# A gated cross-attention stack on one core: scaled scores, the order of the 4-bit minima, a weight split in a tail, and an earlier first query

## The reference, cut to what matters

```
x = x + tanh(g_xattn[i]) * xattn_i(layernorm(x), ctx)
x = x + tanh(g_ffn[i])   * ffn_i(layernorm(x))
```

## Time and profile before

| | |
|---|---|
| median of 3 runs | 2156.29 us (2155.64 to 2157.31) |
| the profiled execution | 2155.29 us; span 2153.5 us from first to last instruction |
| mean granted clock of PE | 0.968 |
| busy, share of the span | PE 92%, DVE 69%, ACT 48%, POOL 44% |
| chain that ended last | PE 64%, DVE 18%, ACT 9%, issue 7%, POOL 1% |
| first layer's attention, loop | about 46 to 588 us |
| third layer's attention | about 1119 to 1490 us |
| third feed-forward | about 1490 to 1524 us |

### The profile page before, as it was taken

The page is one execution under the profiler, slowest core; times in us unless marked ns, Lnnn a source line. Parts: engine busy times, 40 slices in busy tenths (PEclk is TensorE's granted clock), DMA queues, the critical chain, the costliest instruction groups (busy, mean ns, idle before and its releaser), DMA issues.

```text
span 2153.5 us, 33307 instructions
## 1 busy us (share of the span) xinstructions
PE 1971.2 (92%) x10874; PEld 1651.7 (77%) x10874; DVE 1475.5 (69%) x2725; ACT 1029.6 (48%) x2264; POOL 938.5 (44%) x971
## 2 busy tenths in 40 slices
PE   5999999999748999998988999997799999999997
PEld 4788888888636888887666888886678888888886
DVE  5777787777777887887334555656467766677676
ACT  3666666666514544553123544542155555545552
POOL 2555554554445665664321323322144444444432
PEclk9999999999978999999988999999899999999999
DMA  3222221122211111111210101001101110111001
GB/s 140 57 64 75 77 85 57 61 74 67 92 34 40 63 65 54 52 45 64 67 54 4 34 8 34 23 1 55 54 11 47 47 46 11 50 45 45 14 23 45
DMA packets 47070, 106.77 MB, mean 50 GB/s; under 512 B 6065, under 2 KB 21937, under 8 KB 43105
## 3 DMA queue, kind: packets, MB, share of 16 engines
q1 hardware_dynamic: 46944, 105.14, 15.3%
HBM read 98.37 MB, written 6.75 MB: 49 GB/s over the span
## 4 chain that ended last, share of the span: by engine, by line
PE 64%; DVE 18%; ACT 9%; issue 7%; POOL 1%; DVEq 0%; ACTq 0%; POOLq 0%
PE psX L369 23%; PE psQ L369 11%; PE psS L369 11%; PE psO L369 10%; PE psT L752 5%; DVE pT_lo L909 2%; ACT pT_hi L1092 1%; DVE dq_space L461 1%; DVE nmax L897 1%; ACT dq_space L448 1%; DVE p_sb L891 1%; DVE nbias L895 1%; PE psT L369 1%; ACT p_sb L1085 1%; DVE qscr L470 1%
## 5 line engine op out<-in xcount | busy, mean ns | idle before, releaser
L1202 POOL TENSOR_SCALAR p_sb<-p_sb,rrec 128x512 f32<-128x512 f32 (+1 forms) x320 | 266.0, 831 | 704.1 <-DVE rrec L905 704.0
L1092 ACT ACTIVATE pT_hi<-psT 128x512 fp32r<-128x512 f32 (+2 forms) x384 | 235.0, 612 | 336.9 <-PE psT L752 336.0
L909 DVE TENSOR_TENSOR pT_lo<-psT,pT_hi 128x512 fp32r<-128x512 f32 (+2 forms) x384 | 271.4, 707 | 81.9 <-ACT pT_hi L1092 81.9
L369 PE MATMUL psO<-pT_hi,v_hi 128*128 128x256 f32 (+1 forms) x832 | 255.1, 307 | 41.0 <-DVE pT_lo L909 34.1
L752 PE MATMUL psT<-ident,p_sb 128*128 128x128 f32 x1600 | 243.3, 277 | 13.9 <-POOL p_sb L1202 10.5
L369 PE MATMUL psO<-pT_hi,v_lo 128*128 128x256 f32 (+1 forms) x832 | 237.0, 285 | 0.0
L369 PE MATMUL psO<-pT_lo,v_hi 128*128 128x256 f32 (+1 forms) x832 | 237.0, 285 | 0.0
L752 PEld LDWEIGHTS psT<-ident,p_sb 128*128 128x128 f32 x1600 | 195.9, 142 | 53.1 <-POOL p_sb L1202 15.8
L369 PE MATMUL psQ<-xnT_hi,wq_hi 128*128 128x512 f32 (+1 forms) x448 | 189.0, 422 | 18.7 <-DVE qscr L869 9.2
L1085 ACT ACTIVATE p_sb<-psS,nbias 128x512 f32<-128x512 f32 (+1 forms) x192 | 145.3, 757 | 126.6 <-DVE nbias L899 126.6
L369 PEld LDWEIGHTS psO<-pT_hi,v_hi 128*128 128x128 f32 (+1 forms) x832 | 155.0, 186 | 54.2 <-DVE pT_lo L909 45.9
(11 more groups left out here) (337 smaller groups left out, 4786.2 us busy)
## 6 DMA issues: line engine op xcount, KB each, us to landing
wq_f<-in_a_wq SPq DMA_DIRECT2D x96, 256.0 KB, 2.7
wo_f<-in_a_wo SPq DMA_DIRECT2D x24, 1024.0 KB, 6.1
wkv_f<-in_a_wkv SPq DMA_DIRECT2D x24, 512.0 KB, 3.9
mask_sb<-in_codes SPq DMA_DIRECT2D x32, 174.0 KB, 2.4
qscr<-in_amax SPq DMA_DIRECT2D x32, 174.0 KB, 2.3
w<-qscr SPq DMA_DIRECT2D x32, 174.0 KB, 1.9
wo_f<-in_f_wT SPq DMA_DIRECT2D x3, 1024.0 KB, 5.2
wq_f<-in_a_wq SPq DMA_DIRECT2D x16, 192.0 KB, 2.3
```

The lines of the kernel that those rows point to most:

```text
L369: mm = pe.matmul(dst, w, m, start=(first and k == 0), stop=(last and k == n - 1))
L909: L.t_lo.inc(dve.tensor_tensor(pT_view(L, pT_lo, j), t_view(L, j), pT_view(L, pT_hi, j).bitcast(F32), ALU.subtract))
L1092: L.t_hi.inc(act.activation(pT_view(L, pT_hi, j), t_view(L, j), ACT.Copy))
L1202: L.s_norm.inc(pool.tensor_scalar(p_view(L, j), p_view(L, j), rrec[:, j:j + 1], 1.0, ALU.mult, ALU.mult))
```

## The change

- **Scaled scores.** In the first layer the norm's variance is multiplied by the head size before its inverse root is taken, so that the normalised x, which feeds only the queries, comes out divided by sqrt(128). The query biases are scaled once by DVE (a new operation on vecs, 128x32, before the four steps of L995), and ACT waits for it (bq_done) before its first query. In the third layer the query is scaled as it leaves PSUM: a scaled copy on ACT, a three-operand subtraction on DVE. The exponential takes its input unscaled, and the multiplication L899 with its semaphore goes, 128 times in the first layer and 64 times in the third.
- **Minima.** `low` follows directly on `below` and `high` on `above`, ahead of q_low and the drains.
- **Base weights.** `f2_high` on ACT and `f2_low` on POOL split the weights of ffn_2 in four pieces each in the tail of the third layer's attention, in the space of the keys; DVE no longer does. The small expert matrix moves to the space of the values.
- **First query.** PE's wait for the context moves from ahead of the attention to ahead of k0.

```
@@ ln_tile_stats
+            widen = float(layers[0].hd) if k == 0 else 1.0
+            dve.tensor_scalar(ln_var[:, t:t + 1], ln_mv[:, t, 1:2], widen, widen * EPS,
+                              ALU.mult, ALU.add).then_inc(ln_stats, 1)
-            dve.tensor_scalar(ln_var[:, t:t + 1], ln_mv[:, t, 1:2], EPS, None, ALU.add).then_inc(ln_stats, 1)
@@ attn_tensor, use
                 elif kind in "kv":
+                    if L.i == 0 and g is None and what == "k0":
+                        pe.wait_ge(ctx_lo0, 1)
+                        pe.wait_ge(ctx_lo, DC - 1)
@@ attn_vector, row_max
-                    L.s_nm.inc(dve.tensor_reduce(nmax[:, j:j + 1], s_view(L, j), AX.X, ALU.max, negate=True))
-                    L.s_nm.wait(dve, g.at(L.group_slots, k + 1))
-                    L.s_max.inc(dve.tensor_scalar(nbias[:, j:j + 1], nmax[:, j:j + 1], L.scale, None, ALU.mult))
+                    L.s_max.inc(dve.tensor_reduce(nbias[:, j:j + 1], s_view(L, j), AX.X, ALU.max, negate=True))
@@ attn_vector, q_low
-                    ins = dve.tensor_tensor(lo, qscr[:, 0, :] if L.rope else src, hi, ALU.subtract)
+                    ins = dve.scalar_tensor_tensor(lo, src, L.scale, hi, ALU.mult, ALU.subtract)
@@ attn_vector, prologue
                     dve.wait_ge(gate_done, 1)
+                    dve.tensor_scalar(vecs[:, 0:4 * L.n], vecs[:, 0:4 * L.n], L.scale, None, ALU.mult).then_inc(bq_done, 1)
+                    dve.wait_ge(bq_done, 1)
@@ attn_vector, head
                     if L.i == 0 and j in (1, 3):
                         dq_vector(dve, g, h, "below" if j == 1 else "above")
+                        dq_vector(dve, g, h, "low" if j == 1 else "high")
                     if j == L.q_slot[h] and L.head(g, h, L.q_lead):
                         (q_front if L.rope else q_low)(*L.head(g, h, L.q_lead))
...
-                    if L.i == 0 and j in (1, 3):
-                        dq_vector(dve, g, h, "low" if j == 1 else "high")
@@ attn_scalar
-                                           scale=1.0 if L.masked else L.scale, accum_out=rsum[:, j:j + 1]))
+                                           accum_out=rsum[:, j:j + 1]))
...
-                        ins = act.activation(dst, psQ[0:hd, :], ACT.Copy)
+                        ins = act.activation(dst, psQ[0:hd, :], ACT.Copy, scale=L.scale)
...
+                if L.i == 0:
+                    act.wait_ge(bq_done, 1)
                 q_high(Group(0), 0)
...
             def tail(g):
                 o_high(g, 3)
+                if L.i == 2:
+                    f2_high(act, L)
@@ attn_gpsimd, tail
+                elif L.i == 2:
+                    f2_low(pool)
@@ third feed-forward
+        f2_w_hi, f2_w_lo = ([z[:, c // 2, (c % 2) * D:(c % 2 + 1) * D] for c in range(DC)] for z in (kT_hi, kT_lo))
...
-            pe.wait_ge(f2_w, 1)
+            pe.wait_ge(f2_w, DC)
...
+        def f2_high(act, L):
+            act.wait_ge(f2_wdma, 16)
+            L.s_mm.wait(act, L.group_slots * L.n)
+            for c in range(DC):
+                act.activation(f2_w_hi[c], wo_f[:, c, :], ACT.Copy).then_inc(f2_whi, 1)
+
+        def f2_low(pool):
+            for c in range(DC):
+                pool.wait_ge(f2_whi, c + 1)
+                pool.tensor_tensor(f2_w_lo[c], wo_f[:, c, :], f2_w_hi[c].bitcast(F32), ALU.subtract).then_inc(f2_w, 1)
...
         def f2_vector(dve):
-            dve.wait_ge(f2_dma, 16 * 4)
-            dve.tensor_copy(wo_hi[:, :, :], wo_f[:, :, :])
+            dve.wait_ge(f2_dma, 16 * 3)
             after(dve, dve.tensor_copy(f2_b_hi, f2_b_f))
             dve.tensor_tensor(f2_b_lo, f2_b_f, f2_b_hi.bitcast(F32), ALU.subtract)
-            dve.tensor_tensor(wo_lo[:, :, :], wo_f[:, :, :], wo_hi[:, :, :].bitcast(F32), ALU.subtract).then_inc(f2_w, 1)
```

More of the change, by code:

```diff
@@ L162, in __init__ @@
                      wq_hi=4 * n, wq_lo=4 * n, wkv_hi=2 * n, wkv_lo=2 * n, wo_hi=4 * n, wo_lo=4 * n,
-                     q_mm=4 * n, q_hi=4 * n, q_lo=4 * n, s_mm=s, s_nm=0 if self.masked else s,
+                     q_mm=4 * n, q_hi=4 * n, q_lo=4 * n, s_mm=s,
                      s_max=s, s_exp=s, s_rec=s, s_norm=s, t_mm=s, t_hi=s, t_lo=s, av_mm=8 * n, o_hi=4 * n, o_lo=4 * n, x_mm=self.total_x,
@@ L315, in program @@
         vecs = sb("vecs", [P, 64])
-        nmax, nbias, rsum, rrec = (sb(z, [P, 8]) for z in ("nmax", "nbias", "rsum", "rrec"))
+        nbias, rsum, rrec = (sb(z, [P, 8]) for z in ("nbias", "rsum", "rrec"))
         q_ms, q_r, k_ms, k_r = (sb(z, [P, 2, 4]) for z in ("q_ms", "q_r", "k_ms", "k_r"))
@@ L335, in program @@
         x_ready = sem("x_ready")
+        bq_done = sem("bq_done")
         ln_stats, ln_pow, ln_xn, ln_tp, ln_hi, ln_lo = (sem(z) for z in
@@ L348, in program @@
         f1_dhi, f1_dlo = sem("f1_dhi"), sem("f1_dlo")
-        f2_adma, f2_dma, f2_ar, f2_w, f2_h, f2_lg, f2_exp, f2_hw, f2_tp, f2_hwhi, f2_hwlo, f2_out = (
-            sem(f"f2_{z}") for z in ("adma", "dma", "ar", "w", "h", "lg", "exp", "hw", "tp", "hwhi", "hwlo", "out"))
+        f2_adma, f2_wdma, f2_dma, f2_ar, f2_whi, f2_w, f2_h, f2_lg, f2_exp, f2_hw, f2_tp, f2_hwhi, f2_hwlo, f2_out = (
+            sem(f"f2_{z}") for z in ("adma", "wdma", "dma", "ar", "whi", "w", "h", "lg", "exp", "hw", "tp", "hwhi", "hwlo", "out"))
         f3_dma, f3_row, f3_ab, f3_mix, f3_hi, f3_lo, f3_out = (
@@ L1530, in program @@
         ar_f, ar_hi, ar_lo = (z[:, 0:DC * AR] for z in (mask_sb, flat(kx_hi[:, :, :]), flat(kx_lo[:, :, :])))
-        f2_b_f, f2_b_hi, f2_b_lo = qscr[:, 0, :], kT_hi[:, 0, 0:D], kT_lo[:, 0, 0:D]
+        f2_b_f, f2_b_hi, f2_b_lo = qscr[:, 0, :], v_hi[:, 0, 0:D], v_lo[:, 0, 0:D]
+        f2_w_hi, f2_w_lo = ([z[:, c // 2, (c % 2) * D:(c % 2 + 1) * D] for c in range(DC)] for z in (kT_hi, kT_lo))
         def f2_sync(sp, L):
@@ L1546, in f2_tensor @@
                                                    for c in range(DC)]).then_inc(f2_h, 1)
-            pe.wait_ge(f2_w, 1)
+            pe.wait_ge(f2_w, DC)
             for t in range(NT):
-                three(pe, f2_out_banks[t], [(xn_tile(t, c), [z[:, c, :] for z in (wo_hi, wo_lo)]) for c in range(DC)],
+                three(pe, f2_out_banks[t], [(xn_tile(t, c), [f2_w_hi[c], f2_w_lo[c]]) for c in range(DC)],
                       last=False)
```

13 lines of the change are left out of this document (6 added, 7 removed).

## The result

The changed kernel takes **2134.51 us** (median of 4 runs, 2133.57 to 2135.6) against 2156.8 for the kernel before beside it (4 runs): ratio 0.9898, 95% interval 0.9883 to 0.9912. I had forecast 2150.3 and a range down to 2138. The gain is 22 us where I had 6.

A forecast was written before the change was run, and what follows sets the result against it. PE was taken to bound the kernel's first-layer groups. The parts, -0.2 + 2.8 - 1.4 - 7.2 = -6.0 against the profiled 2155.29, gave 2149.3; with the median 1.0 above the profiled run, 2150.3 us, range 2138 to 2156.

The forecast's parts named there:

- Which wait bounds the group: First layer's steady group: PE bounds it; its waits for pT_lo follow from the scores, not from DVE's queue.
- the 4.99 us to PE's start: First layer, from scores done to PE's start after pT_lo: the change can take only the multiplication L899.
- 0.50, 0.64 and 1.18 us: PE's three waits for DVE's pT_lo in a steady first-layer group, 2.3 us in sum.
- DVE's time was the limit after all: Rival: DVE's time limits the first layer, giving -17 there and 2130 in total; chance 0.15.
- The stalls at t0 and t1: First layer, value tile transposes: L974 comes 0.86 us later behind `low` or `high`, so PE waits some 0.9.
- 0.57 and 0.54: First-layer group: psO comes 0.57 us later at the third pT_lo wait, and 0.54 later behind it.
- +0.60 forecast: Net lengthening in us of a first-layer group from the minima back to back, over seven groups +4.2.
- Part 1, -0.2: Scaled scores: removing L899 takes 0.19 us off each first-layer pT_lo wait; 0.4 less 0.2 for the longer first query.
- Part 3, -1.4: First query earlier: v0 starts at 33.0, -1.4 us if the bias scaling waits for POOL, -2.0 if not.
- Part 4, -7.2: Base weights on ACT and POOL: third feed-forward's base matmuls start without the hole, -7.2 us, at worst about -6.
- The clock: Rival, slower: PE's stands at first-layer t0 and t1 drop the granted clock, 2.6 us a fall; chance 0.06.
- the first two waits: First layer: the first two pT_lo waits of a group would be at 0.31 us, shorter by 0.19 and 0.32.

The follow-up runs named there:

- the one that joins all: Changed kernel with the old order of minima, POOL's wkv and wo subtractions one slot later, unread matmuls in the third layer's first and last group: 2123.01 us.
- one kernel's 2.1 us: Changed kernel with `low` or `high` behind the value tile's drain again in slots (2, 3) and (3, 1): 2131.91 us.
- another's 8.1: Changed kernel with L899 back in the third layer alone, scale in the exponential again: 2127.15 us.

## Why the prediction was wrong, point by point

**Which wait bounds the group: the step that failed.** "It is not DVE's queue that is late. The transposes start at 208.55, so the scores are then done, and DVE's maximum starts at that same moment." The coincidence is real and means nothing. The maximum at 208.55 reads the scores that PE had done before those, and they had ended at 206.14; the scores next to the transposes run on until 208.71, after the maximum has started. So the 4.99 us to PE's start did not begin with scores. The last matmul of either, from the timeline of the kernel before:

```profile
205.75 0.39 PE L369 MATMUL psS<-kT_lo,q_hi 128*128 128x512 f32 x1
...
208.32 0.39 PE L369 MATMUL psS<-kT_lo,q_hi 128*128 128x512 f32 x1
```

and the chain that ended last there:

```profile
207.16 1.47 DVE dq_space L461
208.63 0.61 DVE nmax L897
209.26 0.17 DVE nbias L899
```

The maximum waited for the blocked L461 of the earlier trace rows, 1.47 us where 0.51 would do. I had the price of the block, and gave it no place on the path: I took 0.13 for it in one wait. With nearly 1 us less there, the exponential, pT_hi and pT_lo are early enough to take all of the 0.50, 0.64 and 1.18 us. The order alone gave -12.7 in the first layer (I had +2.8 for it), and moving POOL alone -22.4. The rival "DVE's time was the limit after all" (2130, chance 0.15) was the one nearest in time, and even it had the reason only in part: DVE was busy for 52.33 of 67.17 us, and it was the blocked places in its queue, not its total, that were late.

**The stalls at t0 and t1** were right in place and cause, 0.63 each in place of 0.9. But I added their 0.57 and 0.54 to the third wait and behind, because "it hangs on those scores". It hung on the blocked operation ahead of the maximum; with that gone, the chain has room for the late scores, and both terms fall away. Group: +0.60 forecast, -2.08 measured over six groups (93.93 to 484.36 against 97.37 to 500.31: 390.43 and 402.94).

**Part 1, -0.2**, with 0.19 more off each of three waits. The 0.19 was too small: alone the part gave 0.85 a group in place of 0.57, and between the kernel with POOL alone shifted and the one that joins all the group still went from 64.58 to 63.89. Why it is more, no run shows. In the third layer its gain was 0.6 until the last group, and then the clock took 2.8.

**Part 3, -1.4**: right. The first t0 came 0.92 earlier in a trace whose first transposes stand 0.49 later, so -1.4. The choice at the scaling of the biases is decided by its row in the changed kernel's timeline, and POOL's beside it:

```profile
23.62 2.19 POOL L630 TENSOR_TENSOR wkv_lo<-wkv_f,wkv_hi 128x512 fp32r<-128x512 f32 x1 [5.51 <-ACT wkv_hi L618]
...
24.58 1.27 DVE L1000 TENSOR_SCALAR vecs<-vecs 128x32 f32<-128x32 f32 x1
```

A 128x32 operation took 1.27 us: POOL's subtraction had begun at 23.62 and ended at 25.81, and the scaling ended at 25.85, 0.04 behind it. The Trainium skill's rule ("VectorE: DVE Perf Modes", Mode 2×_2P) that such a tensor_scalar takes both port pairs agrees with these two rows. Without the scaling, alone, the part gave -1.7.

**Part 4, -7.2**: right in the third feed-forward, 43.00 to 35.80, with the base product at full clock for 10.97 us (I had 10.9), and the router done in time. That it held is partly luck: with the clock down at its start the same code gives 42.2, a gain of 0.8. The other 0.5 of the stage's -7.7 is the fourth layer's, where nothing was changed.

**The clock.** I had it as a rival with the wrong place (t0 and t1 of the first layer) and a chance of 0.06. There it never fell in a steady group. It fell in the third layer's last group, where the kernels hardly differ in their waits, and cost 2.8; and in the last feed-forward, for 1.6. Neither was in the forecast.

Of the observations that were to prove me wrong, two came: "groups of 65 us", and a span whose gain is not mostly the third feed-forward (7.2 of 21.4 us). Of those that were to show me right, `low` and `high` near 0.81, L974 0.86 later and the waits for scr came too; the first two waits did not stay at 0.31.

## What to carry to other kernels

Two instructions that start at the same time are no evidence of a wait: find the producer's own end, by the slot it works for, and follow the chain back through the queue of the engine itself. Where two engines share a port, an instruction's place in time matters more than its place in the order; before an order on one engine is changed, try to move the other engine's instruction away, which here gave 22.4 us in the first layer, where the whole change gave 18.6, and cost no new wait. And where PE stands for a microsecond or two again and again, compare the granted clock by stage before comparing anything else: useless matmuls in the waits of one group gave 5.4 us, where parts 1 and 3 of the change gave 3.8 and 1.3 alone. Last, give a total to an edit only when the stage that it touches has changed by as much: between profiled runs, 1.6 of one kernel's 2.1 us and 3.7 of another's 8.1 lay elsewhere.

## What the runs showed of the hardware that I had not expected

- The granted clock fell from 1.00 to 0.50 after waits of 1.6 to 2.4 us of PE, although PE worked between them, and whether it fell at a given place differed between kernels which are alike there: one feed-forward took 35.8 or 42.3 us and nothing between. Edits upstream went with it; what decides it is not shown. A gain of a few us in one run of one kernel can be that alone. The spread of 7 to 10 us among runs of some kernels (2134.3 to 2143.3) fits it: the slow run had the lowest mean granted clock each time (0.959 against 0.965 and 0.966 there), though no trace shows where.
- 36 matmuls of 128x512 put into those waits removed all falls in the last group (8.2 us of added PE work at 0.228 each, 5.35 us of time won).
- DVE's 128x348 operation on two operands in SBUF (L461, L467, L471) takes 0.51 us alone, 0.81 behind POOL's normalisation and up to 1.61 behind a weight subtraction, according to who comes first; an operation with its source in PSUM beside POOL's weight subtraction took its 0.74 (L980 at 223.29, POOL's wo_lo from 222.98 to 224.50). The Trainium skill ("SBUF — State Buffer", Who interferes with whom) says both, that the one issued first keeps the shared ports to its end and that a DVE instruction with at most one SBUF input, outside the two-port modes, does not contend; the rows agree.
- DVE stood 2.5 to 3.0 us at the same two places of the fourth layer in fourteen of fifteen traces, ended by nothing that the profile shows ("issue"); it cost PE 1.1 to 2.0 us each time. The cause is open.
